# A two-layer perceiver block on one core: five probability tiles and fewer identity products in the self attentions, identity products in the norms, a context chunk loaded ahead

## What is computed

```python
x = x + L0_xattn(layernorm(x), ctx)          # 16 heads, 4096 context columns
x = x + L0_attn(layernorm(x), wq, wk, wv, wo)  # causal, 16 heads of 32, rope
x = x + L0_ffn(layernorm(x), ...)            # 32 experts + shared, top 6 in 4 of 8 groups
x = x + L1_xattn(layernorm(x), ctx, mask)    # x against 4096 context rows of width 512
x = x + L1_attn(layernorm(x), Wq, ..., key_weights)  # causal, 32 heads of 64, 8 key/value heads
x = x + L1_ffn(layernorm(x), ...)            # 8 experts + shared, top 2, softmax gate

# one self attention, S = 256 tokens
attn = einsum('bhqd,bhkd->bhqk', q, k) * scale      # (L1: times key_weights of the head)
probs = softmax(where(causal, attn, -inf))
out = einsum('bhqk,bhkd->bhqd', probs, v) @ wo.T
```

## Time and profile before

| | us |
|---|---|
| median of 3 executions | 1586.72 (1586.57 to 1587.32) |
| the profiled execution, its own time | 1582.46 |
| its span, first to last instruction | 1580.7 |
| TensorE busy in the span | 1470.3 (93%) |
| VectorE busy | 1150.7 (73%) |
| ScalarE busy | 959.9 (61%) |
| mean granted clock | 0.974 |

### The profile page before, as it was taken

One profiled execution on the slowest core, in us unless ns is written; L12 is line 12 of the kernel. 1 busy time (PEld: TensorE's weight loads), 2 busy tenths in 40 slices (PEclk: granted clock), 3 DMA queues, 4 the chain that ended last, 5 costly groups with the idle time before them and its releaser, 6 DMA issues. The chain is left out here.

```text
span 1580.7 us, 27059 instructions
## 1 busy us (share of the span) xinstructions
PE 1470.3 (93%) x10784; PEld 888.2 (56%) x10784; DVE 1150.7 (73%) x1593; ACT 959.9 (61%) x1755; POOL 108.5 (7%) x99
## 2 busy tenths in 40 slices
PE   2899999999999999994989999999698899997998
PEld 1333333333333333342458999999677645567997
DVE  5999999999999999914465766666565475644665
ACT  0288888888888888882454555555326305534553
POOL 8201110111111111000000000000000000000000
PEclk9999999999999999997998999999899899998999
DMA  7334454444444444164015554544355221001541
GB/s 172 91 64 96 101 147 126 130 126 102 106 106 106 106 106 105 28 87 114 0 35 233 200 183 175 199 175 183 145 241 213 100 113 61 1 1 61 207 180 74
DMA packets 35167, 189.74 MB, mean 120 GB/s; under 512 B 7624, under 2 KB 8048, under 8 KB 23024
## 3 DMA queue, kind: packets, MB, share of 16 engines
q1 hardware_dynamic: 34864, 188.01, 39.6%
q10 hardware_dynamic: 192, 0.20, 0.1%
HBM read 163.50 MB, written 21.54 MB: 117 GB/s over the span
## 5 line engine op out<-in xcount | busy, mean ns | idle before, releaser
L392 DVE TENSOR_REDUCE pm<-bank 128x1 f32<-128x1024 f32 x512 | 621.9, 1223 | 33.3 <-PE bank L468 31.1
L438 ACT ACTIVATE probs<-bank 128x512 f32<-128x512 f32 x1024 | 552.0, 597 | 69.5 <-PE bank L482 10.1
L468 PE MATMUL bank<-kst,qst 50*128 50x512 f32 x1024 | 379.8, 476 | 35.4 <-DMA kst<-kscratch 22.6
L482 PE MATMUL bank<-qst,kst 50*128 50x512 f32 x1024 | 375.9, 453 | 2.6
L495 PE MATMUL bank<-probs,vext 128*32 128x256 f32 x4096 | 327.8, 392 | 1.9
L482 PEld LDWEIGHTS bank<-qst,kst 50*128 50x128 f32 x1024 | 154.8, 186 | 216.3 <-ACT probs L438 193.0
L1035 PE MATMUL bank<-e_xhi,e_hi 128*128 128x256 f32 (+1 forms) x784 | 223.7, 285 | 2.5 <-DVE e_lo L977 2.5
L1035 PE MATMUL bank<-e_xhi,e_lo 128*128 128x256 f32 (+1 forms) x784 | 223.5, 285 | 0.0
L1035 PE MATMUL bank<-e_xlo,e_hi 128*128 128x256 f32 (+1 forms) x784 | 223.4, 285 | 0.0
L495 PEld LDWEIGHTS bank<-probs,vext 128*32 128x32 f32 x4096 | 81.4, 108 | 182.9 <-issue 100.9
L468 PEld LDWEIGHTS bank<-kst,qst 50*128 50x128 f32 x1024 | 151.5, 193 | 55.9 <-DVE pm L392 31.4
(11 more groups left out here) (200 smaller groups left out, 1588.9 us busy)
## 6 DMA issues: line engine op xcount, KB each, us to landing
raw<-wall SPq DMA_DIRECT2D x34, 1536.0 KB, 6.5
kst<-kscratch SPq DMA_DIRECT2D x192, 128.0 KB, 4.3
raw<-wall SPq DMA_DIRECT2D x10, 2304.0 KB, 8.9
kscratch<-ksplit SPq DMA_DIRECT2D x16, 1024.0 KB, 4.4
kraw<-ctx_rows SPq DMA_DIRECT2D x16, 512.0 KB, 4.0
vraw<-ctx_vt SPq DMA_DIRECT2D x16, 512.0 KB, 4.8
ctxT<-ctxT SPq DMA_DIRECT2D x8, 1024.0 KB, 13.4
nat<-ctx_chunks SPq DMA_DIRECT2D x6, 1024.0 KB, 23.2
```

The source lines that it names most:

```text
L392: nc.vector.tensor_reduce(pm[:, h % 2, r % 4, r // 4:r // 4 + 1], bank[:, 2 * (r % 2):2 * (r % 2) + 2, :], AX.XY, ALU.max).then_inc(pre_re ...
L438: nc.scalar.activation(probs[:, (XT * h + n) % PR, :], bank[:, s_bank(h, place(n)), :], ACT.Exp, scale=XSCALE).then_inc(probs_ready, 1)
L468: ins = nc.tensor.matmul(bank[:, 2 * (r % 2) + j, :], qst[64 * j:64 * j + KR, h, tt * P:tt * P + P], kst[64 * j:64 * j + KR, h % 2, c * 51 ...
L482: nc.tensor.matmul(bank[:, s_bank(h, slot), :], kst[64 * j:64 * j + KR, h % 2, m * P:m * P + P], qst[64 * j:64 * j + KR, h, :], start=True ...
```

## The change

`SR` goes from 3 to 5. The identity products of the head loops are issued only in the first five rounds, six in each. `norm_turn_pe` gains eight identity products before its transposes and five after them. In x1 the operands `xhi` and `xlo` are made straight from the two PSUM banks, one token tile at a time. `ctxT[0]` is loaded at the end of e0, and the order of the first three `hi` tiles of `rings0` changes.

```diff
-SR = 3
+SR = 5
...
+def keep_busy(g, times, b):
+
+    wide = g.identb[:, :].unsqueeze(1).to_broadcast([P, 4, P])
+    for i in range(times):
+        g.nc.tensor.matmul(g.bank[:, b, :], g.identb[:, :], wide, start=True, stop=True)
+
+
 def norm_turn_pe(g, pe, k):
+    keep_busy(g, 8, 5)
     for a in range(TA):
         pe.wait_ge(g.xn_ready, TA * k + a + 1)
         for d in range(DC):
             ins = g.nc.tensor.transpose(...)
         ins.then_inc(g.xn_turned, 1)
+    keep_busy(g, 5, 5)
...
             for n in range(heads + SR):
                 if n < heads:
                     scores(n)
-                    keep_busy()
+                    if n < SR:
+                        keep_busy(6)
                 if 0 <= n - SR + 1 < heads:
                     turn_probs(n - SR + 1)
-                    keep_busy()
                 if 0 <= n - SR < heads:
                     values(n - SR)
...
             if later_loads:            # the SP queue of the experts
+                sp.wait_ge(down_done, U * (N - 2))
                 later_loads(sp)
...
-            pe.wait_ge(x_lo, 1)        # cross attention 1
+            pe.wait_ge(x_lo, TA)
...
-            dve.wait_ge(x_hi, 1)
-            nc.vector.tensor_tensor(xlo[:, :, :], g.xnT[:, :, :], xhi[:, :, :].bitcast(F32), ALU.subtract).then_inc(x_lo, 1)
+            for a in range(TA):
+                cols = slice(a * P, a * P + P)
+                dve.wait_ge(g.xnT_ready, TA * (k - 1) + a + 1)
+                nc.vector.tensor_tensor(xlo[:, :, cols], bank[:, 6 + a, :].rearrange("p (d t) -> p d t", d=DC),
+                                        xhi[:, :, cols].bitcast(F32), ALU.subtract).then_inc(x_lo, 1)
...
-            norm_turn_act(g, act, k)
-            act.wait_ge(g.xnT_ready, TA * k)
-            nc.scalar.copy(xhi[:, :, :], g.xnT[:, :, :]).then_inc(x_hi, 1)
+            for a in range(TA):
+                act.wait_ge(g.xn_turned, TA * (k - 1) + a + 1)
+                nc.scalar.copy(xhi[:, :, a * P:a * P + P],
+                               bank[:, 6 + a, :].rearrange("p (d t) -> p d t", d=DC)).then_inc(g.xnT_ready, 1)
...
         def first_d(sp):
-            for c in range(8):
+            for c in range(1, 8):
                 sp.dma_start(ctxT[c][:, :, :], ins["ctxT"][c]).then_inc(ctxT_loaded[c], 16)
+
+        def ahead_d(sp):
+            sp.dma_start(ctxT[0][:, :, :], ins["ctxT"][0]).then_inc(ctxT_loaded[0], 16)
...
-        rings0 = Rings(g, "e0", I0, (69, 81, 93, 57), (105, 117, 129, 141))
+        rings0 = Rings(g, "e0", I0, (81, 93, 69, 57), (105, 117, 129, 141))
...
-                rings0, 4, 4, lambda sp: None, None)
+                rings0, 4, 4, lambda sp: None, ahead_d)
```

More of the change, by code:

```diff
@@ L1224, in cross_attention_1 @@
     nat_loaded = [sem(f"nat_loaded{c}") for c in range(MC)]
-    x_hi = sem("x1_x_hi")
     x_lo = sem("x1_x_lo")
```

## The result

| | before | after |
|---|---|---|
| median, us | 1586.64 (1580.98 to 1587.32, 4 executions) | 1547.3 (1545.97 to 1550.57, 4 executions) |
| ratio of the times, 95% interval | | 0.9768 [0.9749, 0.9787] |
| span of the profiled execution | 1580.7 | 1545.5 |
| mean granted clock | 0.974 | 0.988 |

What follows compares the result with a forecast made beforehand. TensorE was taken as busiest, a third of each head round being unread identity products, plus cold clocks at stage seams. Savings of 18.4 + 5.4 + 1.2 + 3.2 + 6.4 + 1.6 + 2.0 = 38.2 us gave 1548.5, range 1539 to 1564.

Steps and rivals of the forecast that it cites:

- The later rounds: Head loops: 27 rounds of a1 fall from 2.94 to 2.2 us, 11 of a0 from 2.94 to 2.3.
- The chain over two rounds: Head loops: scores, exps, cast or piece, copy, values, next scores take 4.35 us per two rounds in a1, 4.57 in a0.
- The first five rounds: Start of each head loop: rounds with six identity products take 2.24 us; no gain, no loss.
- The ends of the loops: After the last scores round, four turns and five values take 5.3 us instead of 3.6: 1.6 us lost per loop.
- signs of being wrong: Head loops: rounds at a clock under 1.00, values waiting over 0.5 us, or last rounds stretching beyond 5.3 us.
- a0's seam: First products after a0's norm run at full clock: 1.85 us to be had, 1.2 taken.
- e0: Gate and first expert products after the norm run at full clock: 3.2 us saved.
- a1's seam: Start still waits for the bias row; only the clock is gained, 1.6 us.
- x1: Early context chunk starts the first product 4.5 us sooner, clock gives 1.9 of 2.9: together 6.4 us.
- e1: Gate and expert products gain 1.7 us each if the clock holds, which an idle of 2.6 may prevent: 2.0 taken.
- The rival of the norms: Identity products too few, seams stay cold, the five delay what follows: 1561 us; chance 0.2.
- The rival of the cold loops: Clock falls to 0.50 in the head loops, rounds take 4.0 us: about 1616 us; chance 0.07.

Runs made afterwards that it cites:

- copy_first: Changed kernel with ScalarE's copy of the turned probabilities ahead of the wo_high cast and the high_ahead piece: 1544.9 us, 0.9756 of before.
- ids_kept: Changed kernel with two identity products after the scores and two after the turn again in each later head round: 1580.6 us, 0.9975 of before.
- sr3: Changed kernel with three probability tiles instead of five, so six identity products in the first three rounds only: 1542.2 us, 0.9739 of before.
- late_chunk: Changed kernel with ctxT[0] loaded at the start of x1, as before the change: 1557.3 us, 0.9808 of before.
- seams_off: Changed kernel without the eight and five identity products in the norms: 1560.3 us, 0.9841 of before.
- no_ramp: Changed kernel with no identity products in the head loops at all: 1605.7 us, 1.0135 of before.
- burst: Changed kernel without identity products in the first five head rounds, but six once after the scores of head 8: 1558.7 us, 0.9823 of before.
- sr3_copy_two: Changed kernel with three tiles, the copy of turned probabilities first, and two identity products instead of six in the first three rounds: 1547.3 us, 0.9747 of before.
- sr3_copy: Changed kernel with three probability tiles and the copy of turned probabilities ahead of the casts: 1534.8 us, 0.9677 of before.

## Why the prediction was right, and where it was off

- *The later rounds.* The chain over two rounds gave 4.35 in a1 and 4.57 in a0; measured were 4.35 and 4.53. copy_first shows that it is this chain. The gain of the rounds is 27 x (2.94 - 2.17) = 20.8 and 11 x (2.91 - 2.27) = 7.0; the forecast took a0's round before as 2.94, 0.03 too long. ids_kept, which puts the identity products back, is 30.2 us longer in the two stages: it shows that leaving them out is the gain. TensorE's own bound, put at 2.0 to 2.1, is 2.12.
- *The first five rounds.* No gain, no loss: 2.25 a round forecast as 2.24, and scores(5) 11.6 us after scores(0) as before.
- *The ends of the loops*, the term that was mis-sized: 1.6 lost per loop were forecast, 2.4 in a1 (6.05 - 3.6) and 3.0 in a0 (6.63 - 3.6) were measured. The step of 1.13 has the values 0.33 after the turn, and they start 0.48 after it even where they wait for nothing (1.27); nor did it count the first values' wait for ScalarE's copy, 0.26 in a1 and 0.94 in a0. Two of the prediction's own signs of being wrong are thereby met, an end beyond 5.3 us and values that wait longer than 0.5. From scores(0) to the first output product the loops are then 18.3 shorter in a1, for a forecast of 18.4, since the mean round was a little shorter, and 4.0 in a0 instead of 5.4. In sr3 the 2.5 us from the last scores to the first output product are gone: the distance of five makes this loss. The forecast that it saves nothing in the steady state held; what it did not say is that without it the kernel is faster.
- *a0's seam*: the first products are warm, 1.5 (5.5 - 4.0) for a forecast of 1.2. The eight identity products run cold, as said.
- *e0*: 3.7 for 3.2, and 2.2 to 3.7 over the profiles with this code; the full clock holds through the seam.
- *a1's seam*: the start waits for the bias as before, the clock is 1.00. 2.05 (20.35 - 18.3) for 1.6.
- *x1*, also mis-sized: 8.2 for 6.4. The start moved by 4.9, not 4.5, and the clock gave all of its 2.9, not 1.9; the idle before the first product was 1.75 us and not 2.3. 0.4 remain. The second chunk was hidden. late_chunk puts the chunk at 5.7.
- *e1*: 1.8 for 2.0, and that is luck. In this execution the idle of 2.59 did not let the clock fall where the forecast feared it; the gate products were warm, and it fell later, for 3.4 us, so the 1.7 of the expert products was not had. In five of twelve profiles with the same code it fell right behind the idle, and the stage took 149.7 to 149.8, 0.9 more than in before. The fear was right in those, and 2.0 is not a gain that the identity products give each time.
- *The rival of the norms*: seams_off is that case for the clock (the five cold products' delay apart), 1560.3, and 1561 was its price. In e1 alone the rival came true in those five profiles.
- *The rival of the cold loops*: no_ramp is that case. The price of 4.0 a round was 3.83 to 3.88, and 1616 was 1605.7. It was placed on a wrong condition, though: the products of a round hold the full clock well. What decides is whether they begin at it, and the thirty identity products of the first five rounds see to that. With two instead of six in each of three rounds it fell in a0, in some executions.
- *The rule of the Trainium skill* ("TensorE: Matmul & The Clock Gate", Part 4: PE-mode transpose), that the full clock does not engage for transposes: in no_ramp the loop of narrow products and transposes stays at 0.50 over 60 us of unbroken work, in line with it. But in after and burst the same loop holds 1.00 over more than 50 us. So the rule, if it is at work here, bears on the rise of the clock and not on its keeping. And it does not account for the low clock by itself: at the end of the same loops, where the turns are 0.83 of every 2.3 us and not of 3.88, the clock rose to 1.00. What is missing there are the scores. The transposes were not tried apart from the narrow products.

Still open is why one idle is followed by a fall and the next of the same length is not (2.20 us in x1; 2.59 in e1), and what in the first rounds of no_ramp and sr3_copy_two lets the clock fall: in a0 of both it fell before the idle that would explain it, or as that idle began.

## What to carry to other kernels

Products that only keep the clock up belong where it can be lost, ahead of a stretch that idles (a pipeline that fills, a norm), not into each round of a loop that holds it by itself: they cost a quarter of each round here (2.94 against 2.17). A deeper pipeline costs its depth at the end of each loop, so lengthen it only against a wait that the trace shows; a copy that TensorE waits for goes first on its engine. Such products make the full clock likely and not certain (e1). Judge such edits by the stages that they touch, and repeat the executions, for the clock of one program falls in some and not in others.

## What the runs showed of the hardware that was not expected

- The clock stayed at 0.50 over 60 us in which TensorE was busy without a gap (no_ramp). At the loops' ends it rose 4.7 us (a1) and 7.8 us (a0) after the last scores had started, in a stretch of turns and values alone. In burst it rose to 1.00 after one burst of six identity products (2.74 us long at the low clock); the same loop then held 1.00 over 54 us.
- A fall need not come at the idle: in e1 of after it came 5.5 us behind an idle of 2.59, in the midst of dense products, and lasted 3.4 us. In seven other profiles of the same code it came within 1.5 us behind that idle, and lasted 3.4 us in two and 10.2 in five.
- The same idle of 2.20 us in x1 stands in all fourteen profiles. The clock fell at it in eleven, and stayed at 1.00 in seams_off, sr3_copy and sr3_copy_two.
- Cross attention 0 took from 736.3 to 743.7 us with the same code.
